# Image-token chain rewritten: unnormalised norm, squared sum and token scaling on GpSimd

## What is computed

```
probs_t = softmax(q k_t^T * scale)                    # 112 x 371 of each head
text_out = probs_t @ v_t
qsem = l2norm(probs_t @ text)                         # x / max(||x||, EPS), EPS = 1e-12
sem  = qsem @ l2norm(ip)^T                            # 112 x 4
fused = (q k_ip^T) * scale + 0.5 * sem
probs_ip = softmax(fused) * spatial_mask
out = (text_out + probs_ip @ v_ip) @ W_out + b_out + residual
```

## Time and profile before

| | us |
|---|---|
| median of 3 runs | 756.78 |
| lowest, highest | 753.31, 757.88 |
| the profiled execution | 755.47 |
| its span on the core | 753.7 |
| PE busy | 724.7 (96%) |
| DVE busy | 647.0 (86%) |
| ACT busy | 556.2 (74%) |
| POOL busy | 428.7 (57%) |

### The profile page before, as it was taken

How to read it: one execution, slowest core, us unless ns; L and a number is a source line. 1 busy time by engine, 2 the same in 40 slices (tenths; PEclk the granted TensorE clock), 3 DMA queues, 4 the chain that set the end, 5 groups by cost and what they waited for, 6 DMA issues and landing times.

```text
span 753.7 us, 22634 instructions
## 1 busy us (share of the span) xinstructions
PE 724.7 (96%) x7279; PEld 564.7 (75%) x7279; DVE 647.0 (86%) x1860; ACT 556.2 (74%) x1590; POOL 428.7 (57%) x515
## 2 busy tenths in 40 slices
PE   7799999999999999999999999999999999999887
PEld 5477778787877878778787777878777787877664
DVE  4478998989889898988989898899989889898983
ACT  5368687777868778687877878777787878777770
POOL 7245646456564655646565565556656565654653
PEclk9999999999999999999999999999999999999999
DMA  9655362541636345252534436253352624234000
GB/s 262 134 142 109 75 137 63 85 119 37 123 71 122 79 69 131 41 121 72 117 85 59 97 81 126 72 113 82 62 104 72 132 72 85 61 59 103 11 5 17
DMA packets 136195, 67.95 MB, mean 90 GB/s; under 512 B 76320, under 2 KB 136016, under 8 KB 136080
## 3 DMA queue, kind: packets, MB, share of 16 engines
q1 hardware_dynamic: 131504, 63.77, 40.0%
q10 hardware_dynamic: 4576, 2.74, 1.3%
HBM read 39.76 MB, written 15.24 MB: 73 GB/s over the span
## 4 chain that ended last, share of the span: by engine, by line
PE 64%; DVE 15%; issue 7%; POOL 4%; SPq 3%; ACT 3%; DMA 2%; POOLq 0%; DVEq 0%; ACTq 0%
PE ps_gram L742 13%; PE ps_prep L640 12%; PE ps_pT L725 10%; PE ps_gram L743 9%; PE ps_prep L696 5%; PE ps_score L717 4%; PE ps_val L751 3%; DVE pT_lo L1112 3%; DVE low L1107 2%; POOL dual L570 2%; DVE quad_junk L1125 2%; PE ps_prep L790 2%; PE ps_val L752 2%; POOL nrm L577 2%; DVE k_lo L1047 1%
## 5 line engine op out<-in xcount | busy, mean ns | idle before, releaser
L570 POOL TENSOR_TENSOR dual<-prob 128x371 f32<-128x371 f32 (+1 forms) x288 | 253.9, 882 | 295.9 <-ACT prob L940 295.8
L742 PE MATMUL ps_gram<-gram_hi,pT_hi 125*128 125x371 f16 (+1 forms) x864 | 272.3, 320 | 0.1
L743 PE MATMUL ps_gram<-gram_lo,pT_hi 125*128 125x371 f16 (+2 forms) x864 | 230.1, 267 | 0.0
L934 ACT ACTIVATE pT_hi<-ps_pT 125x384 f16<-125x384 f32 (+1 forms) x288 | 139.2, 483 | 108.4 <-PE ps_pT L725 101.6
L924 ACT ACTIVATE prob<-ps_score,low 128x371 f32<-128x371 f32 (+1 forms) x288 | 165.6, 575 | 41.4 <-DVE low L1107 37.5
L1112 DVE TENSOR_TENSOR pT_lo<-ps_pT,pT_hi 125x384 f16<-125x384 f32 (+1 forms) x288 | 155.4, 540 | 33.2 <-ACT pT_hi L934 29.0
L1107 DVE TENSOR_REDUCE low<-ps_score 128x1 f32<-128x371 f32 (+1 forms) x288 | 155.0, 539 | 20.9 <-PE ps_score L717 15.9
L725 PE MATMUL ps_pT<-ident,prob 128*125 128x128 f32 (+1 forms) x864 | 144.0, 275 | 14.3 <-DVE pT_lo L1112 7.6
L1125 DVE CUSTOM_DVE_ANT_0 quad_junk<-ps_gram,dual 128x371 f32<-128x371 f32 (+1 forms) x288 | 153.0, 531 | 3.1 <-issue 0.6
L725 PEld LDWEIGHTS ps_pT<-ident,prob 128*125 128x125 f32 (+1 forms) x864 | 128.8, 187 | 34.3 <-ACT prob L924 15.0
L751 PE MATMUL ps_val<-val,pT_hi 125*128 125x84 f16 (+3 forms) x864 | 152.3, 196 | 0.0
(11 more groups left out here) (200 smaller groups left out, 1481.2 us busy)
## 6 DMA issues: line engine op xcount, KB each, us to landing
ctx_sb<-in_ctx_t SPq DMA_DIRECT2D x15, 750.0 KB, 4.9
w_raw<-k_bounce SPq DMA_DIRECT2D x32, 216.0 KB, 3.9
k_st<-k_bounce SPq DMA_DIRECT2D x28, 216.0 KB, 3.9
k_bounce<-k_hi SPq DMA_DIRECT2D x15, 288.0 KB, 4.3
k_bounce<-k_lo SPq DMA_DIRECT2D x15, 288.0 KB, 4.2
q_st<-q_bounce SPq DMA_DIRECT2D x60, 63.0 KB, 2.5
k_st<-k_hi SPq DMA_DIRECT2D x32, 84.0 KB, 3.2
k_st<-k_lo SPq DMA_DIRECT2D x32, 84.0 KB, 3.6
```

The source lines that it names most:

```text
L570: nc.gpsimd.tensor_tensor(dual[0:r, t % 2, :], prob[0:r, g % 4, 0:TX], prob_16[0:r, t % 2, :], ALU.subtract).then_inc(s_dual, 1)
L742: nc.tensor.matmul(ps_gram[t % 2][:, 0:TX], hi, gh[0:TROWS[i], i, :], start=(i == 0), stop=False, skip_group_check=True)
L743: last = nc.tensor.matmul(ps_gram[t % 2][:, i * TC:TX], hi, gl[0:TROWS[i], i, i * TC:TX], start=False, stop=(i == NT - 1), skip_group_chec ...
```

## The change

The squared norm isn't divided by s^2 any more. POOL squares s (`square_sums`), and DVE forms max(s^2 * EPS^2, p G p) in one operation. The factor 2/G_DOWN moves into the row sum of each block. POOL also multiplies the four products of each head with the inverse norms of the image tokens (`scale_tokens`), which DVE did as k = 6. Since s cancels, the multiplication with 1/s (k = 4) goes too. 1/s itself is still formed, for `text_out`. POOL has to wait for the end of its own addition before it reads `vals`, for which there is a new semaphore, `s_summed`. DVE's list for the chain shrinks from 4 + 13 operations a batch to 2 + 9, and `SOFT_AT` has nine entries.

```diff
-EARLY_VALS_STEP, EARLY_NORM_STEPS, EARLY_POWS = 14, (15, 15, 15, 16), {16: (0, EARLY // 2), 17: (EARLY // 2, EARLY)}
+EARLY_VALS_STEP, EARLY_NORM_STEPS, EARLY_POWS = 14, (15, 15), {16: (0, EARLY // 2), 17: (EARLY // 2, EARLY)}
...
-SOFT_AT = {(1, 0): 0, (1, 1): 1, (1, 2): 2, (2, 0): 3,
-           (4, 0): 4, (4, 1): 5, (4, 2): 6, (5, 0): 7, (5, 1): 8, (5, 2): 9,
-           (7, 0): 10, (7, 1): 11, (7, 2): 12}
+SOFT_AT = {(1, 0): 0, (1, 1): 1,
+           (4, 0): 2, (4, 1): 3, (4, 2): 4, (5, 0): 5,
+           (7, 0): 6, (7, 1): 7, (7, 2): 8}
...
-SOFT_NORMS, SOFT_ARGS = 4, 10
+SOFT_NORMS, SOFT_ARGS = 2, 6
...
+            def square_sums(h0, h1):
+
+                return nc.gpsimd.tensor_tensor(sum_sq[:, h0:h1], vals[:, h0:h1, DH], vals[:, h0:h1, DH], ALU.mult)
+
+            def scale_tokens(f, h0, h1):
+
+                inv = ip_inv[:, :, bass.ds(f.n, 1)].rearrange("s n b -> s b n").to_broadcast([S, h1 - h0, NIP])
+                return nc.gpsimd.tensor_tensor(vals[:, h0:h1, DH + 1:VW], vals[:, h0:h1, DH + 1:VW], inv, ALU.mult)
...
-                    sum_values(0, EARLY).then_inc(s_early, 1)
+                    sum_values(0, EARLY).then_inc(s_summed, 1)
+                    if b.n == 0:
+                        pool.wait_ge(s_setup_ev, 3)
+                    pool.wait_ge(s_summed, 2 * b.n + 1)
+                    square_sums(0, EARLY).then_inc(s_early, 1)
+                    scale_tokens(b, 0, EARLY)
...
-                    sum_values(EARLY, H).then_inc(s_vals, 1)
+                    sum_values(EARLY, H).then_inc(s_summed, 1)
+                    pool.wait_ge(s_summed, 2 * f.n + 2)
+                    square_sums(EARLY, H)
+                    scale_tokens(f, EARLY, H).then_inc(s_vals, 1)
...
-                nc.vector.tensor_tensor_reduce(out=quad_junk[0:r, :], in0=ps_gram[t % 2][0:r, 0:TX], in1=dual[0:r, t % 2, :], scale=1.0,
+                nc.vector.tensor_tensor_reduce(out=quad_junk[0:r, :], in0=ps_gram[t % 2][0:r, 0:TX], in1=dual[0:r, t % 2, :], scale=2.0 / G_DOWN,
...
-                r, n = rsum[:, h0:h1], nrm[:, :, h0:h1]
                 if k == 0:
-                    return nc.vector.reciprocal(r, vals[:, h0:h1, DH])
-                if k == 1:
-                    return nc.vector.tensor_tensor(n[:, 0, :], meta[f.odd][0:S, h0:h1, 0], r, ALU.mult)
-                if k == 2:
-                    return nc.vector.tensor_tensor(n[:, 1, :], n[:, 0, :], r, ALU.mult)
-                return nc.vector.tensor_scalar(n[:, 2, :], n[:, 1, :], 2.0 / G_DOWN, EPS * EPS, ALU.mult, ALU.max)
+                    return nc.vector.reciprocal(rsum[:, h0:h1], vals[:, h0:h1, DH])
+                return nc.vector.scalar_tensor_tensor(out=nrm[:, 0, h0:h1], in0=sum_sq[:, h0:h1], scalar=EPS * EPS,
+                                                      in1=meta[f.odd][0:S, h0:h1, 0], op0=ALU.mult, op1=ALU.max)
...
-                elif k == 4:
+                elif k == 2:
                     dve.wait_ge(s_rn, POWS * (f.n + 1))
                     reached(dve, s_fin_exp, f.n)
-
-                    last = pair(nrm[:, 0, :], nrm[:, 3, :], rsum[:, :], ALU.mult)
-                elif k == 5:
-                    last = pair(fused[:, :, :], vals[:, :, DH + 1:VW], over_ip(nrm[:, 0, :]), ALU.mult)
-                elif k == 6:
-                    inv = ip_inv[:, :, bass.ds(f.n, 1)].rearrange("s n b -> s b n").to_broadcast([S, H, NIP])
-                    last = pair(fused[:, :, :], fused[:, :, :], inv, ALU.mult)
-                elif k == 7:
+                    last = pair(fused[:, :, :], vals[:, :, DH + 1:VW], over_ip(nrm[:, 1, :]), ALU.mult)
+                elif k == 3:
```

More of the change, by code:

```diff
@@ L208, in build @@
         rsum = sb("rsum", [S, H])
-        nrm = sb("nrm", [S, 4, H])
+        sum_sq = sb("sum_sq", [S, H])
+        nrm = sb("nrm", [S, 2, H])
         fused = sb("fused", [S, H, NIP])
@@ L254, in build @@
         s_gram, s_val, s_quad, s_half = sem("s_gram"), sem("s_val"), sem("s_quad"), sem("s_half")
-        s_early = sem("s_early")
+        s_early, s_summed = sem("s_early"), sem("s_summed")
         s_vals, s_chain, s_soft, s_rn = sem("s_vals"), sem("s_chain"), sem("s_soft"), sem("s_rn")
@@ L574, in sum_values @@
                 return nc.gpsimd.tensor_tensor(vals[:, h0:h1, :], raw[0:S, h0:h1, 0:VW], raw[0:S, h0:h1, VW:2 * VW], ALU.add)
+            def square_sums(h0, h1):
[3 more added lines that the diff above has]
+                return nc.gpsimd.tensor_tensor(vals[:, h0:h1, DH + 1:VW], vals[:, h0:h1, DH + 1:VW], inv, ALU.mult)
             def inverse_roots(h0, h1):
-                nc.gpsimd.tensor_tensor(nrm[:, 3, h0:h1], nrm[:, 2, h0:h1], minus_half[0:S, h0:h1], ALU.pow).then_inc(s_rn, 1)
+                nc.gpsimd.tensor_tensor(nrm[:, 1, h0:h1], nrm[:, 0, h0:h1], minus_half[0:S, h0:h1], ALU.pow).then_inc(s_rn, 1)
             def end_early(b, step, prepare):
@@ L1153, in soft @@
                 v, reduce, pair = nc.vector, nc.vector.tensor_reduce, nc.vector.tensor_tensor
-                if k:
+                if k >= SOFT_NORMS:
                     reached(dve, s_soft, SOFT * f.n + k)
@@ L1162, in soft @@
                     last = norms(f, k, EARLY, H)
-                elif k == 4:
+                elif k == 2:
                     dve.wait_ge(s_rn, POWS * (f.n + 1))
                     reached(dve, s_fin_exp, f.n)
-                    last = pair(nrm[:, 0, :], nrm[:, 3, :], rsum[:, :], ALU.mult)
-                elif k == 5:
-                    last = pair(fused[:, :, :], vals[:, :, DH + 1:VW], over_ip(nrm[:, 0, :]), ALU.mult)
-                elif k == 6:
-                    inv = ip_inv[:, :, bass.ds(f.n, 1)].rearrange("s n b -> s b n").to_broadcast([S, H, NIP])
-                    last = pair(fused[:, :, :], fused[:, :, :], inv, ALU.mult)
-                elif k == 7:
+                    last = pair(fused[:, :, :], vals[:, :, DH + 1:VW], over_ip(nrm[:, 1, :]), ALU.mult)
+                elif k == 3:
                     dve.wait_ge(s_ip_score, NB * (f.n + 1))
                     last = pair(fused[:, :, :], fused[:, :, :], meta[f.odd][0:S, :, 1:META], ALU.subtract)
-                elif k == 8:
+                elif k == 4:
                     last = reduce(fmax[:, 0, :], fused[:, :, :], AX.X, ALU.max)
-                elif k == 9:
+                elif k == 5:
                     last = pair(fused[:, :, :], fused[:, :, :], over_ip(fmax[:, 0, :]), ALU.subtract)
-                elif k == 10:
+                elif k == 6:
                     dve.wait_ge(s_fin_exp, f.n + 1)
                     last = reduce(fmax[:, 1, :], fexp[:, :, :], AX.X, ALU.add)
-                elif k == 11:
+                elif k == 7:
                     last = v.reciprocal(fmax[:, 2, :], fmax[:, 1, :])
```

## The result

The changed kernel takes 757.05 us, the median of 22 runs (754.66 to 762.54). The kernel before, run beside it as often, takes 755.45 (752.94 to 759.3). The ratio is 1.0029, with a 95% interval of 1.0016 to 1.0041: slower by 0.3%. The forecast was no change, +2.35 us on the profiled execution, 759.1 as a median, and a range of 748 to 764. The interval tells 0.3% from none here, where the prediction had put that limit at 1%. The profiled execution took 756.85 with a span of 755.0, against 755.47 and 753.7.

What follows compares the result with a forecast made beforehand. PE, 96% busy, was taken as the bound, losing 1.0 us a batch to waits for DVE. Terms +2.5 + 0.5 + 0.15 - 0.8 = +2.35 on 755.47 gave 757.8, as a median 759.1 us; range 748 to 764.

Steps and rivals of the forecast that it cites:

- Part 1: POOL's square and product ahead of `s_vals`: `vals` delayed by 0.55 us, block 3's transposes 0.15 late.
- T3: Start of PE's transposes of block 3 (the number is the block); forecast to come 0.15 us late.
- Part 2: DVE's late norms: the 0.15 us saved is worth nothing, `text_lo` of step 2 waits for block 3's dual.
- L6: Start of the minimum of block 6 in DVE's list; forecast 358.51 against 358.43, 0.08 us later.
- Part 3: Steps 4 and 5: `text_lo` waits for block 5's dual; block 7's transposes at L6 + 6.63, 0.13 us more than the mean.
- Rival 1: `text_lo` of step 4 gets ahead of the dual: 0.45 us gained in 12 batches, median 750.6; chance 0.15.
- Rival 2: DVE gets ahead of the duals in steps 2 and 4, both pauses vanish: batches 43.33, median 743.4; chance 0.10.
- Rival 3: POOL's two operations are long, 1.07 instead of 0.55 us: +9.6 us, median 766.4; chance 0.08.
- Batch 1: Second batch, taken to be like an odd one: loses some 0.5 us.
- Batch 14: Batch with preparation but no text to split: only the new wait before block 3's transposes, 0.15 us.
- The last batch: No preparation on PE, waits run through DVE, so removed work counts: -0.8 us, between 0 and -1.9.
- The tail: POOL's 0.45 to 0.55 us added, L1167's and L1172's waits go or move: 0, between -0.6 and +0.3.

Runs made afterwards that it cites:

- The kernel with the delay alone: Kernel before, plus two unused POOL operations and the wait for its own addition ahead of `s_vals`, late part only: 757.3 us, ratio 1.0041.
- the early signal (first experiment): Changed kernel, but the late addition itself raises `s_vals`; square and product raise their own semaphore, awaited one DVE operation later: 754.07 us, ratio 0.9995.

## Why the prediction was right, and where it wasn't

**Part 1** forecast a delay of 0.55, taken between 0.40 and 1.07. From the start of the late addition to the reciprocal it was 0.45 before (352.71 to 353.16) and is 0.93 now (353.40 to 354.33): 0.48. The wait of POOL for its own end is the part that was too large: 353.89 - 353.81 = 0.08, not 0.25. T3 was to come 0.15 late; it comes 0.03 and 0.16 late. The two experiments on the delay show the cause by taking it away and by putting it in alone.

**Part 2** forecast that `text_lo` of step 2 runs into the dual of block 3 and that L6 comes 0.08 later. It takes 0.72 and 0.84, and from the batch's start to L6 it is 17.22 in batch 7 against 17.18, and in batch 8 0.15 more than before. The sign and the mechanism held, the mean is 0.10. The kernel with the delay alone has the same L6, so the delay makes all of it by itself; without the delay the rewrite has L6 0.07 earlier than before.

**Part 3** forecast 0.7 to 0.8 for the operation in L1167's place (0.78), 1.0 for `text_lo` of step 4 (1.03), T7 at L6 + 6.63 (6.56 and 6.62) and all batches alike at 44.5 (44.56 and 44.45 in turn, mean 44.50). Per batch it is +0.17 rather than +0.21, over twelve batches +2.1 rather than +2.5. Rival 1 had `text_lo` ahead of the dual, for a batch less by 0.45. It didn't happen by itself. In the experiment that moves it there a batch takes 0.10 less than before, not 0.45. T7 is then at L6 + 6.31 on average, not + 5.97: L1187 waits next (0.52), and the rival's own sum took L1172 off batch 7's 6.17 and left out the reduction (0.15) and the larger operation in L1167's place (0.78 for 0.72), which part 3 itself counts. Rival 2's 43.33 a batch is there to be had as well, not by removing work but by moving `text_lo` out of the duals' way. Rival 3 fell with the delay of 0.48.

**Batch 1** is the term that was wrong: +0.5 forecast, 0.0 measured. The pause before T7 did grow, by 0.39. But another one shrank, at T1, which comes 6.41 behind the batch's start instead of 6.83; at T3 0.37 of that is left. The timeline of DVE and PE there, before:

```profile
80.68 0.88 DVE L1138 TENSOR_SCALAR nrm<-nrm 112x14 f32<-112x14 f32 x1
...
81.93 0.54 DVE L1112 TENSOR_TENSOR pT_lo<-ps_pT,pT_hi 125x384 f16<-125x384 f32 x1
...
82.61 0.56 PE L725 MATMUL ps_pT<-ident,prob 128*125 128x128 f32 x3 [0.59 <-ACT prob L924]
```
and changed:

```profile
81.56 0.56 DVE L1130 TENSOR_TENSOR pT_lo<-ps_pT,pT_hi 125x384 f16<-125x384 f32 x1 [0.23 <-ACT pT_hi L952]
...
82.27 0.56 PE L743 MATMUL ps_pT<-ident,prob 128*125 128x128 f32 x3 [0.16 <-DVE pT_lo L1130]
```
Before, the last of the four early operations on the norms (L1138) stood ahead of the minimum and of `pT_lo` of block 0, and took 0.88. `pT_lo` ended at 82.47 and T1 started at 82.61. The view names ScalarE; it was DVE, as with T5. Now the operation is gone, and `pT_lo` starts 5.70 behind the batch's start instead of 6.15, held by ScalarE alone. The experiments bear it out: with the delay alone, and so with the four early operations, T1 is at 6.84, with the rewrite and the early signal at 6.40. The step that failed is my sentence that the early operations cost nothing since PE has no pause in those steps. That holds in the batches that I had looked at, and not in batch 1. Busy time in two stretches, of batches 1 and 2, before (stretch, its length, busy us of PE, PEld, DVE, ACT, POOL, then the granted clock, DMA share, GB/s):

```profile
75.00:86.00 11.00, 10.33 (x131) 8.44 (x128) 9.70 (x30) 7.84 (x25) 8.22 (x9) 1.00 0.24 36
119.00:130.00 11.00, 11.00 (x136) 9.55 (x134) 10.00 (x31) 7.80 (x24) 7.04 (x7) 1.00 0.37 102
```
and batch 1, changed:

```profile
75.00:86.00 11.00, 10.70 (x136) 8.74 (x133) 9.50 (x28) 7.70 (x26) 8.88 (x12) 1.00 0.29 53
```
PE is busy for 11.00 of 11.00 us in batch 2 already before, so nothing can be won there. In batch 1 it goes from 10.33 to 10.70.

**Batch 14** was to be +0.15 and is +0.22. **The last batch** was to be -0.8: from its first score to POOL's late addition it is 42.41 (696.96 to 739.37) against 43.26 (694.56 to 737.82), -0.85. The gain comes in three places: T2 is 0.38 earlier behind the batch's start (the early L1138 again, 0.88 before), T5 0.68 (L1137's 0.90 is gone), T9 0.84. **The tail** was to be 0 between -0.6 and +0.3. From the addition to the first operation behind the power (L1167, now L1180) it is 3.73 against 3.25, +0.48, and from there to the maximum 1.03 against 1.57, -0.54: together -0.06. Start and batch 0 together are +0.1. The sum of the trace is +0.1 + 0.0 + 2.1 + 0.2 - 1.0 = +1.4 (1.3 by the unrounded spans), against +2.35: 0.5 less by batch 1, 0.4 less by twelve batches. The median forecast was 2.1 too high, and 1.3 of that is another matter: it set the median of before 1.3 above the profiled execution, by three runs, and over 22 runs it stands at 755.45, level with it.

## What to carry to other kernels

Where two engines exclude each other, a removed operation isn't worth its busy time: DVE lost 20.7 us of busy time here and the kernel got no faster, because the next operation with two inputs in SBUF took the place in front of the same lock; with the late signal on top it got 0.3% slower. List the starts of both engines' operations side by side, see who comes first and by how much, and move the one that loses (1.5% for one line of a table, which moved ScalarE's halves with it) before taking work away. Raise a signal with the operation whose result is waited for: two small ones ahead of it cost 2 us here.

## What the runs showed of the hardware beyond that

**The clock in the tail.** The chain of waits ends with PE's last products. The chain of the changed kernel (start, us, engine, output, line):

```profile
748.67 1.04 PE ps_score L874 x4
749.71 1.60 PE ps_prep L808 x6
```
and the stretch around it, columns as above:

```profile
745.00:751.00 6.00, 4.16 (x18) 2.67 (x19) 2.08 (x6) 0.45 (x1) 0.00 (x0) 0.81 0.00 0
```
With the early signal (first experiment), the same:

```profile
746.98 0.99 PE ps_prep L808 x6
```
and

```profile
744.00:748.90 4.90, 3.61 (x21) 2.19 (x20) 1.76 (x4) 0.45 (x1) 0.00 (x0) 1.00 0.00 0
```
Six products took 1.60 us in one and 0.99 in the other. The granted clock was 0.81 over the stretch in one and 1.00 in the other; of its two levels the second is 2.4 GHz throughout, and the first is a mixture with 1.2. PE had pauses between short groups of work in both. The kernel before had the 1.60 too. From the start of the `ps_score` group to the end of the `ps_prep` group behind these six it was 3.44 in one and 2.04 in the other, 1.4 us. The engine's records don't say why one run keeps the clock for longer.

**The start.** Batch 0 began between 28.93 and 35.48 us in the eleven profiled executions, although the setup differs in none of them. In the two latest (34.93 and 35.48) the granted clock was 0.66 and 0.67 between 10 and 20 us; in the other nine it was 1.00 there. Several microseconds between two single profiles are thus no difference between two kernels, and batches have to be compared from start to start.

**A small wait.** POOL's wait for its own last operation cost 0.08 us in mid-batch, not the 0.25 of the one row in the setup.
